# Local attention on one core: score tiles with 128 stationary columns in place of 82

## The chip, the cores and the metric

The kernel runs on one core of a Trainium2 chip. The metric is the device time of one execution in microseconds (us), as a median of repeated runs. A profiler's trace of one further execution shows what each engine did. The engines are TensorE (matmuls, PE in the profile, with its weight loads as PEld), VectorE (DVE), ScalarE (ACT), GpSimd (POOL) and SyncE (SP), which issues transfers.

A matmul on TensorE has two operands: the stationary one, which a weight load puts into the array of 128 rows by 128 columns, and the moving one, which is then streamed through column by column. In the profile a form such as `32*82 32x146` is a stationary operand of 32 rows and 82 columns and a moving one of 32 rows and 146 columns. Stationary columns become partitions of the result in PSUM. Where the operands have only 32 rows, a matmul uses one of four row strips of the array, and matmuls on different strips can run side by side.

## The reference

32 images and texts are embedded to 164 tokens each (36 of the image by a stem and a deformable convolution, 128 of the text by a quantized table), of width 192. Then comes one layer of local attention with 12 heads of 16, and a two-layer spline network. The attention is what the change touches:

```python
q = (x @ Wq + bq).reshape(B, N, H, d).transpose(0, 2, 1, 3)
k = (x @ Wk + bk).reshape(B, N, H, d).transpose(0, 2, 1, 3)
v = (x @ Wv + bv).reshape(B, N, H, d).transpose(0, 2, 1, 3)
scores = jnp.einsum('bhqd,bhkd->bhqk', q, k) * SCALE
allowed = jnp.abs(idx[:, None] - idx[None, :]) <= 64
scores = jnp.where(allowed[None, None], scores, -jnp.inf)
attn = jax.nn.softmax(scores, axis=-1)
out = jnp.einsum('bhqk,bhkd->bhqd', attn, v)
...
h = h + out @ Wo + bo
```

## The kernel before

The program has three stages that follow each other on the core: the tokens (stem, offsets, sampling, deformable convolution, text), the attention (`attend_phase`) and the spline network. The change is in the second, with some constants that the first loads and casts.

The attention works on pairs of sequences, 16 pairs, with a loop body for an even and an odd pair. A sequence's 164 tokens are split into two halves of 82 (`ROWS`). As a token sees at most 64 neighbours to each side, a half needs 82 + 64 = 146 (`SPAN`) columns on the other side of its scores. The 12 heads lie as 4 row strips of 32 partitions (j) times 3 groups (`HG`, g). Queries and keys are split into a high and a low part of type F32R (four bytes), so that scores need two passes: against `k1` and `k2`.

For each sequence TensorE computes the scores twice:

- by query (`queries_scores`), into the PSUM tile `scores_by_query` of two banks, in four blocks q = 0 to 3. A block covers one half of the tokens and two strips (strips 0 and 1 for even q, 2 and 3 for odd q): 12 matmuls that stream 146 columns (L1329), then 6 that add the mask (`add_mask`, L1352, which streams 96, 96 and 108 columns on each strip). VectorE then takes the maximum over the keys (L1021). There is one such tile: the next block waits until the maximum has read it.
- by key (`keys_scores`), into `scores_by_key` of four banks, in two blocks c = 0, 1. A block covers one half of the tokens and all four strips: 24 matmuls (L1364), 12 for the mask (L1352) and 12 that subtract the queries' maxima (L1374, with the stationary constant `pickr` and the moving transposed maxima `mT`). ScalarE then exponentiates (L1194).

The other matmuls of a round are the transposes of x and of the maxima (L1294, L1384), the projections to queries, keys and values (L1301 to L1305, L1313 to L1317), the weighted sums (`mix`, L1396) and the output projection (L1408). The order on TensorE is written out by hand in `pair`: while one sequence's scores by key are made, the next sequence's scores by query are made between them. In the first half of a pair's loop body (i = 0) the next pair's x is transposed and its queries and keys are projected; in the second half (i = 1) its values are. VectorE in the second half computes the layer statistics of the pair after the next (`norm_in`) ahead of the first maximum. `keep_going` issues matmuls whose result is not used, at the start and the end of the stage.

The stationary operands of the touched matmuls are 82 columns of `q1` (L1329), of `k1` and `k2` (L1364), of `piecer` (L1352) and all of `pickr` (L1374). Results lie on 82 partitions, and VectorE and ScalarE read these.

At the stage's start GpSimd fills buffers with constants (L978 to L983); each memset counts up `zeros_set`, and TensorE, VectorE, ScalarE and GpSimd wait for 6 of these. The constants `piece` and `pick` come by transfer in the first stage and are cast to F32R by VectorE (L470, L472).

Of the kernel before, what the change touches and what calls it, by code (L numbers as in the profile page):

```python
# [19 lines left out]
F32 = mybir.dt.float32  # L20
F32R = mybir.dt.float32r
# [4 lines left out]
P = 128  # L26
# [11 lines left out]
TOK = VIS + TXT  # L38
ROWS = TOK // 2
WINDOW = 64  # L40
SPAN = ROWS + WINDOW
# [3 lines left out]
PT = 2 * TOK  # L45
# [9 lines left out]
HEADS, DH = 12, 16  # L55
HG = HEADS // 4
# [56 lines left out]
class Constants:  # L113
# [4 lines left out]
    def __init__(self, nc, stack, a, front):  # L118
        sb, ps, sem = memories(nc, stack)
        self.pix_neg = sb("pixel_neg", [P, NPIXC + 1])  # L120
        self.ident = front.ident
        self.rows = sb("deform_rows", [P, 2, D])
        sizes = (("wq", HG * P), ("wk", HG * P), ("wv", D))
        self.high = [sb(f"attend_{k}_high", [P, 2, n], F32R) for k, n in sizes]
        self.low = [sb(f"attend_{k}_low", [P, 2, n], F32R) for k, n in sizes]
        self.piecer = sb("window_piece_r", [P, 2, SPAN], F32R)
        self.maskr = sb("window_mask_r", [P, 2, EDGE], F32R)
        self.pickr = sb("attend_pick_r", [P, HG, ROWS], F32R)
        self.minus_low = sb("attend_minus_low", [P, 2])
        self.xe = sb("attend_x_rest_ones", [P, PT], F32R)  # L130
        self.offset_in, self.pixel_in, self.attend_in = sem("offset_in"), sem("pixel_in"), sem("attend_const_in")
        self.dcn_in = sem("deform_in")

    def stage(self, nc, stack, a):

        sb = memories(nc, stack)[0]
        sizes = (("wq", HG * P), ("wk", HG * P), ("wv", D))
        self.off_w = sb("offset_weights", [P, TAPS, 2 * TAPS])
        self.off_bias = sb("offset_bias", [P, 1])
        self.off_grid = sb("offset_grid", [P, 8 * VIS])  # L140
        self.raw = [sb(f"attend_{k}", [P, 3, n]) for k, n in sizes]
        self.rest_low = sb("attend_rest_low", [P, 1])
        self.piece = sb("window_piece", [P, 2, SPAN])
        self.mask = sb("window_mask", [P, 2, EDGE])
        self.pick = sb("attend_pick", [P, HG, ROWS])
        self.ones_row = sb("attend_ones_row", [P, PT])
        self.loads = ((self.off_w[0:C1], a["off_w"], self.offset_in), (self.off_bias[:], a["off_bias"], self.offset_in),
                      (self.off_grid[:], a["off_grid"], self.offset_in), (self.ident[:], a["identity"], self.offset_in),
                      (self.pix_neg[0:PIXC], a["pix_neg"], self.pixel_in),
                      *((dst[:], a[k], self.attend_in) for dst, k in  # L150
                        ((self.raw[0], "wq"), (self.raw[1], "wk"), (self.raw[2], "wv"), (self.rest_low, "rest_low"), (self.mask, "mask"), (self.piece, "piece"), (self.pick, "pick"),
                         (self.minus_low, "minus_low"))))
        self.attend_count = 16 * (len(self.loads) - self.FIRST)
        self.loads += self.more
# [660 lines left out]
def attend_phase(nc, c, front, a, vis_scr, txt_scr, h_scr, w_raw, w1_in, total_scr, rec_scr):  # L815
# [14 lines left out]
    with ExitStack() as stack:  # L830
# [13 lines left out]
        q1, k1, k2 = ([sb(f"attend_{k}{u}", [P, HG, PT], F32R) for u in range(2)] for k in ("q1_", "k1_", "k2_"))  # L844
# [131 lines left out]
        def _(pool):  # L976
# [3 lines left out]
            pool.memset(prT[0:ROWS, 0, :, SPAN:TOK], 0.0).then_inc(zeros_set, 1)  # L980
            for u in range(2):
                pool.memset(va[u][:, :, :, 0:DH], 0.0).then_inc(zeros_set, 1)
                pool.memset(va[u][:, :, :, DH:32], 1.0).then_inc(zeros_set, 1)  # L983
            pool.wait_ge(half_set, 1)
            pool.wait_ge(zeros_set, 6)
# [14 lines left out]
        def _(dve):  # L1000
            dve.wait_ge(zeros_set, 6)
# [157 lines left out]
        def _(act):  # L1159
# [88 lines left out]
            act.wait_ge(zeros_set, 6)  # L1248
# [20 lines left out]
        def _(pe):  # L1269
# [49 lines left out]

            def queries_scores(a, u, i, q, first=False):  # L1320
# [4 lines left out]
                for g in range(HG):  # L1325
                    for k in (k1[u], k2[u]):
                        for j in range(2):
                            r = slice(64 * h + 32 * j, 64 * h + 32 * j + 32)
                            nc.tensor.matmul(sc[0:ROWS, j, g * SPAN:(g + 1) * SPAN],  # L1329
                                             q1[u][r, g, i * TOK + n * ROWS:i * TOK + (n + 1) * ROWS],  # L1330
# [4 lines left out]
            def add_mask(scores, n, tiles, stop):  # L1335

                for p in range(3):
                    for row, bank in tiles:
                        r = slice(32 * row, 32 * row + 32)
                        of = scores[0:ROWS, bank, 0:SW].rearrange("p (g n) -> p g n", n=SPAN)  # L1340
# [11 lines left out]
                        last = nc.tensor.matmul(to, piecer[r, n, at:at + ROWS], edge, start=False,  # L1352
# [3 lines left out]
            def keys_scores(a, u, i, c, most, first=False):  # L1356
# [3 lines left out]
                for g in range(HG):  # L1360
                    for k in (k1[u], k2[u]):
                        for j in range(4):
                            r = slice(32 * j, 32 * j + 32)
                            nc.tensor.matmul(tp[0:ROWS, j, g * SPAN:(g + 1) * SPAN],  # L1364
                                             k[r, g, i * TOK + c * ROWS:i * TOK + (c + 1) * ROWS],
                                             q1[u][r, g, i * TOK + FROM[c]:i * TOK + FROM[c] + SPAN],
                                             start=(g == 0 and k is k1[u]), stop=False)
# [3 lines left out]
                for g in range(HG):  # L1371
                    for j in range(4):
                        r = slice(32 * j, 32 * j + 32)
                        last = nc.tensor.matmul(tp[0:ROWS, j, g * SPAN:(g + 1) * SPAN], pickr[r, g, :],  # L1374
# [101 lines left out]
            pe.wait_ge(zeros_set, 6)  # L1476
# [505 lines left out]
def layouts(i):  # L1982
# [55 lines left out]
    for j, (conv, bn) in enumerate((("stem", "bn1"), ("dcn", "bn2"))):  # L2038
# [11 lines left out]
        "pick": np.tile(-(row % DH == group).astype(f32)[..., None], (1, 1, ROWS)),  # L2050
# [4 lines left out]
        "piece": np.tile(np.stack([piece, piece[:, ::-1]], 1).astype(f32), (4, 1, 1)),  # L2055
# [25 lines left out]
```

## Time and profile before

| what | value |
|---|---|
| median of 3 runs | 2442.05 us (2440.94 to 2452.29) |
| the profiled execution | 2410.74 us, its span 2409.0 us |
| mean granted TensorE clock | 0.974 |
| TensorE matmuls busy | 2301.1 us (96%), 19971 instructions |
| weight loads busy | 2153.2 us (89%) |
| VectorE busy | 1878.0 us (78%) |
| ScalarE busy | 1397.2 us (58%) |
| GpSimd busy | 229.8 us (10%) |

The span runs from the first to the last instruction of the program, and the profiled execution's own time is 1.7 us longer. Busy times are unions of the instructions' intervals; since matmuls are pipelined and overlap, a busy TensorE is not one at its peak, and the pace is read from the starts of instructions that follow each other. The granted clock is the share of TensorE's full clock that its throttle let through. A wait is written behind the instruction that it held up, with what ended it.

### The profile page before, as it was taken

To read this page: it belongs to the slowest core of one execution; us is meant where nothing else is said; L and a number is where in the kernel's file an instruction comes from. 1 tells how busy PE (TensorE), PEld (TensorE's weight loads), DVE (VectorE), ACT (ScalarE), POOL (GpSimd) and SP (SyncE) were. 2 spreads that over 40 slices of the span, in tenths; PEclk is the share of its full clock that TensorE was granted. 3 is DMA by queue.
4 is the path that set the end of the run, shared out by engine and by line. 5 is a ranking of instruction groups with operands and counts; after the bars stand their busy time and mean duration, and the time that the engine had idled before them with its cause. 6 is when DMAs were issued, how large, how long until landed. Compare 5 with 4: busy or idle time off the path is not lost.

```text
span 2409.0 us, 48738 instructions
## 1 busy us (share of the span) xinstructions
PE 2301.1 (96%) x19971; PEld 2153.2 (89%) x19971; DVE 1878.0 (78%) x2364; ACT 1397.2 (58%) x1391; POOL 229.8 (10%) x133
## 2 busy tenths in 40 slices
PE   7699989999999889999999999989999999999999
PEld 6466877777777789999999999989999999999999
DVE  8799755666666487766766767689999999999995
ACT  5689113444444554435435344588888888888881
POOL 5522000000000021211211111000000000000000
PEclk9899997999999899999999999999999999999999
DMA  7655131111111100000000000210000000000000
GB/s 238 178 149 152 47 142 34 45 47 44 47 47 44 37 22 27 20 15 26 20 24 19 19 26 24 90 59 23 24 22 23 23 23 23 23 23 23 23 19 10
DMA packets 99326, 115.82 MB, mean 48 GB/s; under 512 B 15271, under 2 KB 90551, under 8 KB 98487
## 3 DMA queue, kind: packets, MB, share of 16 engines
q1 hardware_dynamic: 79087, 89.38, 12.3%
q10 hardware_dynamic: 16520, 14.34, 2.0%
q0 software_dynamic: 3616, 10.54, 1.7%
q8 instruction: 87, 1.43, 0.2%
q14 instruction: 16, 0.13, 0.0%
HBM read 83.36 MB, written 30.86 MB: 47 GB/s over the span
## 4 chain that ended last, share of the span: by engine, by line
PE 64%; issue 0%; DVE 0%
PE spline_acc L1915 27%; PE spline_acc L1888 10%; PE spline_acc L1887 10%; PE spline_acc L1889 10%; PE spline_acc L1909 5%; PE spline_acc L1911 2%; PE spline_xT L764 0%; DVE spline_f L1664 0%; DVE spline_weights_low L1647 0%; DVE spline_x L1734 0%; DVE spline_x L1737 0%
## 5 line engine op out<-in xcount | busy, mean ns | idle before, releaser
L1915 PE MATMUL spline_acc<-spline_weights,spline_f 128*128 128x192 f32 x3936 | 672.2, 328 | 0.0
L1915 PEld LDWEIGHTS spline_acc<-spline_weights,spline_f 128*128 128x128 f32 x3936 | 637.4, 190 | 0.0
L1887 PE MATMUL spline_acc<-spline_f,spline_weights_high 128*128 128x328 f32 x1536 | 480.5, 313 | 2.5 <-DVE spline_weights_low L1647 2.5
L1888 PE MATMUL spline_acc<-spline_f,spline_weights_high 128*128 128x328 f32 x1536 | 481.2, 313 | 0.0
L1889 PE MATMUL spline_acc<-spline_f,spline_weights_low 128*128 128x328 f32 x1536 | 477.7, 311 | 0.0
L1887 PEld LDWEIGHTS spline_acc<-spline_f,spline_weights_high 128*128 128x128 f32 x1536 | 289.1, 188 | 2.8 <-DVE spline_weights_low L1647 2.8
L1889 PEld LDWEIGHTS spline_acc<-spline_f,spline_weights_low 128*128 128x128 f32 x1536 | 289.3, 188 | 0.0
L1888 PEld LDWEIGHTS spline_acc<-spline_f,spline_weights_high 128*128 128x128 f32 x1536 | 289.3, 188 | 0.0
L1909 PE MATMUL spline_acc<-spline_weights_split,spline_f_high 128*128 128x384 f32 x656 | 218.2, 389 | 8.2 <-issue 8.2
L1664 DVE SCALAR_TENSOR_TENSOR spline_f<-spline_front 128x984 fp32r<-128x984 f32 x128 | 145.6, 1178 | 100.2 <-PE spline_acc L1889 94.9
L1021 DVE TENSOR_REDUCE attend_max<-scores_by_query 82x6 f32<-82x876 f32 x128 | 136.3, 1065 | 57.5 <-PE scores_by_query L1352 56.8
L1817 ACT ACTIVATE spline_hid<-spline_acc 128x328 f32<-128x328 f32 x64 | 28.2, 445 | 243.6 <-PE spline_acc L1889 243.6
L1911 PE MATMUL spline_acc<-spline_weights_split,spline_f_low 128*128 128x192 f32 x656 | 164.6, 251 | 0.0
L1194 ACT ACTIVATE attend_probs<-scores_by_key 82x1752 f32<-82x1752 f32 x64 | 104.3, 1630 | 93.2 <-PE scores_by_key L1374 93.2
L1664 DVE SCALAR_TENSOR_TENSOR spline_f<-spline_n,spline_a 128x984 fp32r<-128x984 f32 x64 | 75.6, 1181 | 99.7 <-PE spline_acc L1889 98.9
L1675 DVE SCALAR_TENSOR_TENSOR spline_f<-spline_front 128x1536 f32<-128x1536 f32 x84 | 147.0, 1750 | 0.0
L1675 DVE SCALAR_TENSOR_TENSOR spline_f<-spline_n,spline_b 128x1536 f32<-128x1536 f32 x80 | 140.0, 1750 | 0.0
L1909 PEld LDWEIGHTS spline_acc<-spline_weights_split,spline_f_high 128*128 128x128 f32 x656 | 124.0, 189 | 8.5 <-issue 8.5
L1911 PEld LDWEIGHTS spline_acc<-spline_weights_split,spline_f_low 128*128 128x128 f32 x656 | 125.7, 192 | 0.0
L574 ACT ACTIVATE spline_front<-spline_front,pixel_neg 120x576 f32<-120x576 f32 x160 | 109.7, 763 | 12.4 <-DMA spline_front<-pos_scr 11.1
L1782 ACT ACTIVATE spline_s<-spline_xn,spline_offset 128x512 f32<-128x512 f32 x160 | 101.9, 708 | 7.9 <-DMA spline_xn<-hid_scr 6.4
L1329 PEld LDWEIGHTS scores_by_query<-attend_k,attend_q 32*82 32x82 f32 x1536 | 69.6, 154 | 41.0 <-DVE attend_max L1021 25.2
(229 smaller groups left out, 4266.6 us busy)
## 6 DMA issues: line engine op xcount, KB each, us to landing
spline_front<-pos_scr SPq DMA_DIRECT2D x32, 540.0 KB, 4.4
hid_scr<-spline_hid SPq DMA_DIRECT2D x64, 164.0 KB, 1.8
spline_xn<-hid_scr SPq DMA_DIRECT2D x41, 256.0 KB, 3.1
attend_spread<-rec_scr SPq DMA_DIRECT2D x128, 61.5 KB, 2.1
pix_scr<-spline_front SPq DMA_DIRECT2D x32, 225.0 KB, 3.8
spline_weights_raw<-w SPq DMA_DIRECT2D x1, 6144.0 KB, 21.4
spline_weights<-w SPq DMA_DIRECT2D x4, 1536.0 KB, 6.2
spline_x<-h_scr SPq DMA_DIRECT2D x41, 96.0 KB, 1.9
```

The source lines that it names most:

```text
L574: nc.scalar.activation(dy[u][0:PIXC, part, :].rearrange("p (k n) -> p k n", k=TAPS), p[:, 0], ACT.Abs, bias=neg[0:PIXC, part:part + 1])
L1021: nc.vector.tensor_reduce(mx[0:ROWS, n, 2 * h:2 * h + 2, 0:HG], sc[0:ROWS, :, 0:SW].rearrange("p j (g n) -> p j g n", n=SPAN), AX_X, ALU.m ...
L1194: nc.scalar.activation(prT[0:ROWS, c, :, FROM[c]:FROM[c] + SPAN].rearrange("p (j g) n -> p j g n", j=4), tp[0:ROWS, :, 0:SW].rearrange("p ...
L1664: nc.vector.scalar_tensor_tensor(f[j % RING][:, part * HC:(part + 1) * HC], n_[u][:, cols], MAGIC + i, v[:, cols], ALU.is_equal, ALU.mult) ...
L1675: nc.vector.scalar_tensor_tensor(dst[:], n, MAGIC + i, v, ALU.is_equal, ALU.mult).then_inc(f_ready, 1)
L1782: nc.scalar.activation(dst[:, r * HID:(r + 1) * HID].rearrange("p (c n) -> p c n", c=CH), x2[u], ACT.Identity, bias=bias2[:, r:r + 1], sca ...
L1887: nc.tensor.matmul(z, high, x_high, start=start, stop=False)
L1888: nc.tensor.matmul(z, high, x_low, start=False, stop=False)
L1889: last = nc.tensor.matmul(z, low, x_high, start=False, stop=stop)
L1909: nc.tensor.matmul(acc2[:, u, 0:2 * D], f_high[i][:, cols], w2_split[:, i, r].rearrange("p s o -> p (s o)"), start=start, stop=False)
L1911: last = nc.tensor.matmul(z, f_low[i][:, cols], w2_split[:, i, r, 0, :], start=False, stop=False)
L1915: last = nc.tensor.matmul(z, f_rest[i][:, cols], w2[:, i, r, :], start=False, stop=stop)
```

## The change

The stationary operands of all score, mask and maximum matmuls grow from 82 to 128 columns. What is streamed stays. The results have 46 more partitions, which nobody reads. As the 128 columns from the last position of a buffer would reach past its end, `q1`, `k1` and `k2` (two buffers each) get 46 further columns behind their three groups; elsewhere the further columns are those of the neighbouring tokens or of the next group. The tails are filled with zeros by six more memsets on GpSimd, and the waits on `zeros_set` go from 6 to 12. `piecer` grows from 146 to 192 columns a half, padded with zeros, and `pickr` from 82 to 128 a group.

```diff
-        self.piecer = sb("window_piece_r", [P, 2, SPAN], F32R)
+        self.piecer = sb("window_piece_r", [P, 2, WINDOW + P], F32R)
-        self.pickr = sb("attend_pick_r", [P, HG, ROWS], F32R)
+        self.pickr = sb("attend_pick_r", [P, HG, P], F32R)
...
-        q1, k1, k2 = ([sb(f"attend_{k}{u}", [P, HG, PT], F32R) for u in range(2)] for k in ("q1_", "k1_", "k2_"))
+        wide = {k: [sb(f"attend_{k}{u}", [P, HG * PT + P - ROWS], F32R) for u in range(2)] for k in ("q1_", "k1_", "k2_")}
+        q1, k1, k2 = ([y[:, 0:HG * PT].rearrange("p (g n) -> p g n", g=HG) for y in wide[k]] for k in ("q1_", "k1_", "k2_"))
...
+            for y in wide["q1_"] + wide["k1_"] + wide["k2_"]:
+                pool.memset(y[:, HG * PT:].bitcast(F32), 0.0).then_inc(zeros_set, 1)
...
-            pool.wait_ge(zeros_set, 6)
+            pool.wait_ge(zeros_set, 12)
...
+            def columns(k, u, r, g, at):
+
+                at += g * PT
+                return wide[k][u][r, at:at + P]
+
...
-                            nc.tensor.matmul(sc[0:ROWS, j, g * SPAN:(g + 1) * SPAN],
-                                             q1[u][r, g, i * TOK + n * ROWS:i * TOK + (n + 1) * ROWS],
+                            nc.tensor.matmul(sc[:, j, g * SPAN:(g + 1) * SPAN],
+                                             columns("q1_", u, r, g, i * TOK + n * ROWS),
...
-                        last = nc.tensor.matmul(to, piecer[r, n, at:at + ROWS], edge, start=False,
+                        last = nc.tensor.matmul(to, piecer[r, n, at:at + P], edge, start=False,
...
-                            nc.tensor.matmul(tp[0:ROWS, j, g * SPAN:(g + 1) * SPAN],
-                                             k[r, g, i * TOK + c * ROWS:i * TOK + (c + 1) * ROWS],
+                            nc.tensor.matmul(tp[:, j, g * SPAN:(g + 1) * SPAN],
+                                             columns(k, u, r, g, i * TOK + c * ROWS),
...
-                        last = nc.tensor.matmul(tp[0:ROWS, j, g * SPAN:(g + 1) * SPAN], pickr[r, g, :],
+                        last = nc.tensor.matmul(tp[:, j, g * SPAN:(g + 1) * SPAN], pickr[r, g, :],
```

## Rows read from the trace of the kernel before

**Rows 1.** Busy time by window: the attention stage; columns: us, busy (x instructions), granted clock, DMA.

```profile
337.00:838.00 501.00, 461.61 (x8261) 392.35 (x8257) 307.98 (x674) 208.34 (x302) 17.03 (x17) 0.93 0.15 42
```

**Rows 2.** The same view: one round at full clock, one with a half-clock stretch.

```profile
591.40:620.60 29.20, 27.11 (x519) 23.16 (x518) 19.65 (x44) 12.93 (x19) 1.00 (x1) 1.00 0.17 47
558.10:591.40 33.30, 31.42 (x520) 26.48 (x519) 19.68 (x45) 12.92 (x19) 1.00 (x1) 0.85 0.16 41
```

**Rows 3.** Groups of weight loads by shape: count | busy us, mean ns | idle before.

```profile
L1329 PEld LDWEIGHTS scores_by_query<-attend_k,attend_q 32*82 32x82 f32 x1536 | 69.6, 154 | 41.0 <-DVE attend_max L1021 25.2 <-issue 15.7
...
L1352 PEld LDWEIGHTS scores_by_query<-window_mask_r,window_piece_r 32*82 32x82 f32 x768 | 40.4, 154 | 0.0
L1364 PEld LDWEIGHTS scores_by_key<-attend_q,attend_k 32*82 32x82 f32 x1536 | 39.4, 157 | 8.8 <-issue 3.9 <-ACT attend_probs L1194 1.9
...
L1352 PEld LDWEIGHTS scores_by_key<-window_mask_r,window_piece_r 32*82 32x82 f32 x768 | 24.7, 160 | 0.0
L1374 PEld LDWEIGHTS scores_by_key<-attend_max_split,attend_pick_r 32*82 32x82 f32 x768 | 24.5, 159 | 4.8 <-DVE attend_max_split L1035 4.6
```

**Rows 4.** Timeline of weight loads, a key and a query block: start, us.

```profile
646.17 0.52 PEld L1364 LDWEIGHTS scores_by_key<-attend_q,attend_k 32*82 32x82 f32 x24 [0.20 <-issue]
646.60 0.30 PEld L1352 LDWEIGHTS scores_by_key<-window_mask_r,window_piece_r 32*82 32x82 f32 x12
...
647.32 0.54 PEld L1329 LDWEIGHTS scores_by_query<-attend_k,attend_q 32*82 32x82 f32 x12 [0.19 <-issue]
647.75 0.33 PEld L1352 LDWEIGHTS scores_by_query<-window_mask_r,window_piece_r 32*82 32x82 f32 x6
```

**Rows 5.** The same timeline: loads of 128 and of 82 columns following each other.

```profile
643.13 0.19 PEld L1301 LDWEIGHTS attend_spare<-attend_x_high,attend_wk_high 128*128 128x128 f32 x1 [0.65 <-ACT attend_mixed L1187]
643.24 0.19 PEld L1302 LDWEIGHTS attend_spare<-attend_x_low,attend_wk_high 128*128 128x128 f32 x1
...
653.76 0.15 PEld L1313 LDWEIGHTS attend_spare<-attend_wv_high,attend_x_high 128*82 128x82 f32 x1
653.83 0.15 PEld L1314 LDWEIGHTS attend_spare<-attend_wv_low,attend_x_high 128*82 128x82 f32 x1
653.92 0.15 PEld L1315 LDWEIGHTS attend_spare<-attend_wv_high,attend_x_low 128*82 128x82 f32 x1
...
671.80 0.20 PEld L1384 LDWEIGHTS attend_spare<-identity_all,attend_max 82*128 82x128 f32 x2 [0.23 <-issue]
```

**Rows 6.** Timeline of weight loads at half clock.

```profile
566.44 0.54 PEld L1352 LDWEIGHTS scores_by_query<-window_mask_r,window_piece_r 32*82 32x82 f32 x6
```

**Rows 7.** Timeline of TensorE's matmuls: the waits of one round.

```profile
650.94 0.66 PE L1329 MATMUL scores_by_query<-attend_k,attend_q 32*82 32x146 f32 x12 [0.61 <-DVE attend_max L1021]
...
652.97 0.66 PE L1329 MATMUL scores_by_query<-attend_k,attend_q 32*82 32x146 f32 x12 [0.27 <-DVE attend_max L1021]
...
659.79 0.45 PE L1374 MATMUL scores_by_key<-attend_max_split,attend_pick_r 32*82 32x146 f32 x12 [0.25 <-DVE attend_max_split L1035]
...
666.66 0.39 PE L1301 MATMUL attend_spare<-attend_x_high,attend_wq_high 128*128 128x328 f32 x1 [0.49 <-DVE attend_x_rest L1044]
```

**Rows 8.** Timeline of VectorE in the same round.

```profile
649.82 1.07 DVE L1021 TENSOR_REDUCE attend_max<-scores_by_query 82x6 f32<-82x876 f32 x1
```

**Rows 9.** Busy time by window: before and in a half-clock stretch.

```profile
558.00:562.00 4.00, 3.08 (x88) 2.56 (x86) 2.69 (x4) 0.99 (x1) 1.00 (x1) 1.00 0.25 68
562.00:572.00 10.00, 10.00 (x128) 8.06 (x124) 4.76 (x13) 2.39 (x5) 0.00 (x0) 0.50 0.14 44
```

**Rows 10.** Timeline of all engines at the stage's start.

```profile
314.92 0.74 POOL L983 MEMSET attend_v<- 128x768 f32 x1
...
319.62 1.14 DVE L668 BATCH_NORM_STATS2 attend_stats<-attend_x 82x6 f32<-82x192 f32 x4 [9.47 <-DMA attend_x<-txt_scr]
```

**Rows 11.** Timeline of VectorE where the constants are cast.

```profile
64.49 0.31 DVE L470 CAST window_piece_r<-window_piece 128x292 fp32r<-128x292 f32 x1 [3.55 <-DMA attend_minus_low<-minus_low]
...
69.86 0.52 DVE L480 SCALAR_TENSOR_TENSOR spline_front<-offset_acc,offset_bias,offset_grid 128x288 f32<-128x288 f32 x1 [1.20 <-PE offset_acc L447]
```

More of the change, by code:

```diff
@@ L142, in stage @@
         self.rest_low = sb("attend_rest_low", [P, 1])
-        self.piece = sb("window_piece", [P, 2, SPAN])
+        self.piece = sb("window_piece", [P, 2, WINDOW + P])
         self.mask = sb("window_mask", [P, 2, EDGE])
-        self.pick = sb("attend_pick", [P, HG, ROWS])
+        self.pick = sb("attend_pick", [P, HG, P])
         self.ones_row = sb("attend_ones_row", [P, PT])
@@ L1000, in _ @@
         def _(dve):
-            dve.wait_ge(zeros_set, 6)
+            dve.wait_ge(zeros_set, 12)
             def norm_in(tt, u):
@@ L1247, in _ @@
                 high(k1[0][:, g, :], start(START["K"][g]))
-            act.wait_ge(zeros_set, 6)
+            act.wait_ge(zeros_set, 12)
             for i in range(2):
@@ L1339, in add_mask @@
                         r = slice(32 * row, 32 * row + 32)
-                        of = scores[0:ROWS, bank, 0:SW].rearrange("p (g n) -> p g n", n=SPAN)
+                        of = scores[:, bank, 0:SW].rearrange("p (g n) -> p g n", n=SPAN)
                         if p < 2:
@@ L1360, in keys_scores @@
                 for g in range(HG):
-                    for k in (k1[u], k2[u]):
+                    for k in ("k1_", "k2_"):
                         for j in range(4):
                             r = slice(32 * j, 32 * j + 32)
-                            nc.tensor.matmul(tp[0:ROWS, j, g * SPAN:(g + 1) * SPAN],
-                                             k[r, g, i * TOK + c * ROWS:i * TOK + (c + 1) * ROWS],
+                            nc.tensor.matmul(tp[:, j, g * SPAN:(g + 1) * SPAN],
+                                             columns(k, u, r, g, i * TOK + c * ROWS),
                                              q1[u][r, g, i * TOK + FROM[c]:i * TOK + FROM[c] + SPAN],
-                                             start=(g == 0 and k is k1[u]), stop=False)
+                                             start=(g == 0 and k == "k1_"), stop=False)
                 add_mask(tp, c, [(j, j) for j in range(4)], False)
@@ L1475, in _ @@
             keep_going(48, tp[:, 0, 0:HG * P])
-            pe.wait_ge(zeros_set, 6)
+            pe.wait_ge(zeros_set, 12)
             for j in range(2):
@@ L2049, in layouts @@
         "wo": wo.reshape(P, HG, D),
-        "pick": np.tile(-(row % DH == group).astype(f32)[..., None], (1, 1, ROWS)),
+        "pick": np.tile(-(row % DH == group).astype(f32)[..., None], (1, 1, P)),
         "minus_low": -np.concatenate([row % 32 >= DH, row % 32 >= DH], 1).astype(f32),
@@ L2054, in layouts @@
         "mask": np.tile(np.where(np.stack([mask, mirror], 1), NEG, 0.0).astype(f32), (4, 1, 1)),
-        "piece": np.tile(np.stack([piece, piece[:, ::-1]], 1).astype(f32), (4, 1, 1)),
+        "piece": np.tile(np.pad(np.stack([piece, piece[:, ::-1]], 1), ((0, 0), (0, 0), (0, P - ROWS))).astype(f32), (4, 1, 1)),
         "patches": x.reshape(B, 3, HS, K, HS, K).transpose(1, 3, 5, 0, 2, 4).reshape(PATCH, B, PIX),
```

## The prediction, made before the result was known

> **What bounds the kernel now.** The page of the profile comes first: TensorE is busy for 96% of the span, and the chain that ended last runs almost wholly through its matmuls. The change touches one stage alone, so I cut the span into stages and look at the windows: from 337 to 838 us the attention runs, 501 us long, with TensorE busy for 462 of them, VectorE for 308 and ScalarE for 208 [rows 1]. The other two stages keep their instructions, apart from the preparations costed below.
>
> Next, one steady round of the stage's loop, a pair of sequences of 164 tokens: 29.20 us at the full clock, 33.30 us where a stretch at half clock fell into it [rows 2]. The reader is to see that the same 519 or 520 instructions take 4.1 us more there.
>
> Then the weight loads of the touched lines by shape [rows 3]. The five groups hold 1536 + 768 + 1536 + 768 + 768 loads, all of 32 rows by 82 columns. Queries' scores use two row strips of the array at once, keys' scores four. I call one load on each strip in use a step: 1536/2 + 768/2 + 1536/4 + 768/4 + 768/4 = 1920 steps, 60 for each of 32 sequences: four query blocks of 9 steps and two key blocks of 12.
>
> How long is a step? In the load timeline, L1364's 24 loads (6 steps) begin at 646.17 and L1352's at 646.60: 72 ns a step. L1329's 12 loads (6 steps) begin at 647.32, L1352's at 647.75: 72 ns again, with half as many strips [rows 4]. The mask steps, whose matmuls stream 96 or 108 columns and not 146, are no shorter: six loads take 0.33 us from the first's start to the last's end, one takes 0.15, and the 0.18 between are two steps and the offset of the second strip [rows 4, 5]. At half clock the same 6 mask loads take 0.54 [rows 6]. So a step does not follow what is streamed; it follows something that halves with the clock and is the same for 96 and 146 columns. The load itself is the candidate.
>
> **What a load of 128 columns costs.** Where nothing streams yet and two loads follow each other, the second begins as soon as the first lets it. With 82 columns that is 0.07 us (653.76 to 653.83); with 128 columns, of the same four-byte type as the changed tiles, 0.11 us (643.13 to 643.24) [rows 5]. These are loads on all 128 rows, the nearest rows there are; the trace has no load of 32 rows by 128 columns. The 0.07 agrees with the 72 ns of a strip's step, so I take the same difference for the strips: +0.04 us a step. Scaling 72 ns by 128/82 gives 112, the same 0.04. At half clock it is 0.08. The other bound is zero or a gain: two loads of 128 columns for a transpose (L1384) fit into 0.20 us, where the pair at 643.13 needs 0.11 + 0.19 = 0.30 [rows 5]. That is a transposing matmul on plain F32; the changed ones are ordinary matmuls on F32R, as the pair at 643.13, so I go with the latter.
>
> The Trainium skill speaks against this: its page "TensorE: Matmul & The Clock Gate", section on weight-path perf modes, says that fast weight load comes on when there are exactly 128 weights and the type is not FP32. The same section grants no win to 32-bit weights. The F32R loads at 643.13, 0.11 us apart, do not show it at work; no run here shows it on strips of 32 rows. By that rule the sum would be that of the first rival below, and not the one that follows.
>
> **The sum.** All 1920 steps at +0.04 are 77 us. What of it is on the path is read from one round, engine by engine.
>
> *Second sequence's half, from 646.17.* The first key block (12 steps, +0.48) and first query block (9, +0.36) end before the next query block, which starts at 650.94 after 0.61 us idle, released by VectorE's maximum [rows 7]. That maximum began only at 649.82, 1.7 us after the scores it reads were streamed at about 648.1; VectorE had the next pair's layer statistics to do first [rows 4, 8]. In between stands the output projection, which ends 0.61 us before 650.94. The scores can come 0.84 later. The projection slips by 0.84 less the 0.19 that the loads at 647.32 stood idle [rows 4]: 0.65 against 0.61, so nothing worth counting is late. If that cover were gone, 0.65 us a round. The later three query blocks are in line with everything: 3 x 0.36. The second key block runs while VectorE takes the maximum of block two; TensorE waits 0.27 us for that anyway, at 652.97, and part of the block runs on strips the queries do not use [rows 7]. Its release is already late by the 0.36 counted, so of 0.48 I count nothing. Sum 1.08.
>
> *First sequence's half.* The key block waits 0.25 us (TensorE) for the split maxima at 659.79 [rows 7]; its nine steps before that (+0.36) overrun the wait by 0.11 at most, which I leave to the range. Its three steps after it: 0.12. Four query blocks 4 x 0.36 = 1.44, second key block 0.48. Against it the wait of 0.49 for VectorE's low part of x at 666.66 goes [rows 7]: VectorE's chain to it moves by 0.36 (through one maximum), TensorE by 0.84. Sum 0.12 + 1.44 + 0.48 - 0.49 = 1.55.
>
> Together 2.63 of 4.80 us a round, 55%; 16 rounds make 42 us. The four query blocks ahead of the first round (+1.4) and the three that the last one lacks (-1.1) cancel.
>
> *The clock.* The stage's mean granted clock is 0.93 [rows 1]; with the two levels 1.0 and 0.5 that is 14% of 501 us, 70 us, at half clock. A stretch of 10 us there holds 128 matmuls [rows 9], against 519 in 29.20 [rows 2]: 0.72 of the pace, so 10% of the steps, 192. There TensorE is busy for 10.00 of 10, and each step costs 0.08, uncovered: 15 us. The other nine tenths: 0.9 x 42 = 38. Sum 53 if the falls stay as they are. The two in steady rounds begin at about 562 and 743; the first follows a stretch in which TensorE was busy for only 3.08 of 4 us [rows 9], the second looks alike; most of the missing time is the wait for the maximum, which the change fills. I take it that these two go: 2 x 4.1 back, and their 20 of the 70 us cost 4 less. **53 - 8 - 4 = +41 us.**
>
> *The rest.* Six more memsets of 46 columns on GpSimd stand ahead of the release of all engines (12 counts in place of 6). The last of today's begins at 314.92 and takes 0.74; VectorE waits until 319.62 for x by DMA [rows 10], 4 us of cover for what a memset of 768 columns sets at 0.74 each, six of 46 at well under 1 us in all. Two constants grow, 292 to 384 and 246 to 384 columns (118 KB more by DMA), and their casts (0.31 for 292 columns) by some 0.2; VectorE idles 1.20 us for TensorE soon after [rows 11]. Both cost nothing; uncovered, about 1 us each. Matmul counts, streamed columns, semaphores and what the other engines read stay.
>
> **The rivals.** *A fast load.* If strips load 128 columns in under 0.07, streaming sets the step. Matmuls of 192 columns follow at 0.09 (653.83 to 653.92) [rows 5], 0.47 ns a column: 68 ns for 146, 45 for 96, 51 for 108. A query block then takes 549 in place of 657 ns, a key block 753 in place of 876: 1.36 a round, 12 us at the 55% above, 22 at all of it, and up to 8 more from the falls. Middle -20: 2422 us. For it speaks L1384, against it L1301. It decides from the point where the load is shorter than today's 72 ns.
>
> *The clock stays full all through.* 70 us at half clock cost 0.41 of their length by [rows 2] (4.1 of 10), 29 us; 42 - 29 = +13: 2455. For it: the waits get filled. Against: some stretches fall outside steady rounds.
>
> *Nothing hides.* Maximum and projection chains slip with TensorE, or falls come oftener (4.1 each): 0.9 x 77 + 15 = +84: 2526.
>
> *The step is not the load's* but a fixed cost of a strip: 0, 2442. Against it stands that 0.07 and 0.11 differ at all.
>
> **How the numbers follow.** The profiled execution took 2410.74 us, 31.3 less than the median 2442.05; I carry the difference of +41 over: 2483. Chances: load-bound and half hidden (+20 to +65) 0.63; nothing hides 0.11; clock stays full 0.10; fast load 0.10; no change 0.06. Half a per cent, 12 us, is about what a measurement of this kernel can tell from none. Slower: the first two and a little of the third, 0.76; same: no change and half of the clock's, 0.12; faster: 0.12. The range leaves out the fast load, the case of no change and the top of "nothing hides": 2447 to 2520.
>
> **What the profile would show.** Right: touched loads 0.11 apart, key steps at 646 to 647 stretched by half; rounds of 31.8 us in place of 29.2; waits before L1329 and L1301 shorter; the stage near 540 us, the others as before. Wrong: steps still 72 ns or less, rounds shorter than 29.2, or the stage's mean clock at 1.0.

## The result, and the profile after

| | before | after |
|---|---|---|
| median of 6 runs | 2439.78 us (2412.88 to 2452.29) | 2516.70 us (2507.41 to 2532.74) |
| the profiled execution, its span | 2410.74, 2409.0 us | 2532.74, 2531.1 us |
| its mean granted clock | 0.974 | 0.943 |

The ratio is 1.0354 (95% interval 1.0308 to 1.0399): slower, as forecast, and inside the range; but the medians moved by 77 us where 41 were forecast. The ratio compares the fast runs of the two kernels alone and is not the quotient of the two medians (1.0315).

First the step. In the timeline of the weight loads of the kernel after (start, us, engine, line, then the tiles), the 24 loads of the keys' scores (now L1372) begin at 533.01 and the mask's at 533.68: 0.67 us for 6 steps, 0.11 a step where [rows 4] have 0.07.

```profile
524.25 0.74 PEld L1337 LDWEIGHTS scores_by_query<-attend_k,attend_q 32*128 32x128 f32 x12 [0.44 <-DVE attend_max L1024]
...
526.62 0.74 PEld L1337 LDWEIGHTS scores_by_query<-attend_k,attend_q 32*128 32x128 f32 x12
527.28 0.41 PEld L1360 LDWEIGHTS scores_by_query<-window_mask_r,window_piece_r 32*128 32x128 f32 x6
...
533.01 0.75 PEld L1372 LDWEIGHTS scores_by_key<-attend_q,attend_k 32*128 32x128 f32 x24
533.68 0.42 PEld L1360 LDWEIGHTS scores_by_key<-window_mask_r,window_piece_r 32*128 32x128 f32 x12
...
571.87 1.40 PEld L1337 LDWEIGHTS scores_by_query<-attend_k,attend_q 32*128 32x128 f32 x12
573.15 0.76 PEld L1360 LDWEIGHTS scores_by_query<-window_mask_r,window_piece_r 32*128 32x128 f32 x6
```

Two strips at 526.62 (queries, now L1337) give 0.66 for 6 steps, the same 0.11. At half clock, from 571.87, they take 1.28: 0.21 a step. The same block at half clock in the kernel before takes 0.84, 0.14 a step, so there the change costs 0.07 a step:

```profile
383.91 0.96 PEld L1329 LDWEIGHTS scores_by_query<-attend_k,attend_q 32*82 32x82 f32 x12
384.75 0.54 PEld L1352 LDWEIGHTS scores_by_query<-window_mask_r,window_piece_r 32*82 32x82 f32 x6
```

Now the rounds, in the view of busy time by window (us, then PE, PEld, DVE, ACT and POOL busy with their instructions, granted clock, DMA): ten steady rounds; one at full clock; the next; and in that one the stretch before its fall of the clock, and the fall. Last, all that lies ahead of the attention.

```profile
523.13:881.43 358.30, 350.04 (x5182) 306.82 (x5181) 198.70 (x431) 129.11 (x190) 10.02 (x10) 0.88 0.14 38
523.13:555.17 32.04, 31.21 (x521) 27.65 (x520) 19.95 (x45) 12.92 (x19) 1.00 (x1) 1.00 0.15 43
555.17:594.83 39.66, 38.79 (x519) 33.69 (x518) 19.79 (x45) 12.91 (x19) 1.00 (x1) 0.78 0.13 35
555.20:559.60 4.40, 4.25 (x90) 3.88 (x88) 2.60 (x4) 0.70 (x1) 1.00 (x1) 1.00 0.36 90
559.60:576.70 17.10, 17.10 (x169) 14.50 (x168) 6.13 (x14) 4.30 (x6) 0.00 (x0) 0.50 0.10 29
0.00:355.00 355.00, 295.27 (x1635) 212.61 (x1637) 277.27 (x359) 192.19 (x306) 120.95 (x92) 0.92 0.53 152
```

The same ten rounds and the same first 355 us of the kernel before:

```profile
470.33:771.99 301.66, 279.92 (x5182) 238.37 (x5181) 196.79 (x432) 129.26 (x190) 10.04 (x10) 0.97 0.17 46
...
0.00:355.00 355.00, 306.20 (x1845) 227.69 (x1846) 287.04 (x384) 194.28 (x308) 101.49 (x87) 0.95 0.54 154
```

A full-clock round takes 32.04 us, 2.84 more than the 29.20 of [rows 2]. But every other round takes 39.66, since the clock falls to half for 17.1 us in it. The falls of the ten rounds begin at 559.6, 631.3, 703.0, 774.7 and 846.3: 71.7 apart, which is one round of each kind. Before, two stretches of 10 us fell into ten rounds, at 4.1 each. So of the 56.6 us that ten rounds gained (358.30 less 301.66), 28.4 are ten full-clock rounds' 2.84, and the clock's share is 5 x 7.62 less 2 x 4.1, 30; the two make 58. The whole stage, from the first query scores to the last weighted sums, went from 493.1 us (336.5 to 829.6) to 598.8 (354.6 to 953.3), where the prediction's sum gave some 40 more.

What stands ahead of a fall is new too. In [rows 9] TensorE was busy for 3.08 of the 4 us before it; here for 4.25 of 4.40. Its timeline shows, behind the output projection that ends at 556.1, query block, key block and query block with no gap but 0.15:

```profile
556.29 0.89 PE L1337 MATMUL scores_by_query<-attend_k,attend_q 32*128 32x146 f32 x12 [0.15 <-DVE attend_max L1024]
...
558.66 0.89 PE L1337 MATMUL scores_by_query<-attend_k,attend_q 32*128 32x146 f32 x12
559.40 0.60 PE L1360 MATMUL scores_by_query<-window_mask_r,window_piece_r 32*128 32x96 f32 x6
559.93 0.45 PE L1316 MATMUL attend_spare<-attend_wv_high,attend_x_high 128*82 128x192 f32 x1
```

The Trainium skill, page "TensorE: Matmul & The Clock Gate", section "HAM oscillation — how this bites in real kernels", describes a kernel whose clock falls in TensorE's waits for transfers between bursts of matmuls. No such wait stands ahead of this fall: the wait of 0.61 is down to 0.15, and the fall comes all the same.

**How much of the 77 is the clock.** Executions of one kernel differ mainly in it. The 47 runs of the kernel before that stand beside this study's runs reach from clock 0.960 to 0.975; with an execution's half-clock time taken as 2 x (1 - clock) x span, a straight line through them costs 0.41 us per us of it (the clock is given to 0.001, which is 5 us). Their median, 0.967, is 160 us at half clock; the six runs of after have 0.9495, 254 us. So 94 x 0.41 = 38 us of the 77 are clock, and 39 are left for the loads. This is an estimate: the line is carried on from at most some 195 us at half clock to 254, though the six runs of after, taken alone, give 0.415 too. Against the 47 runs' own median time, 2435.5 us, the difference is 81, and 43 are left; 16 rounds of 2.84 are 45.

The profiled executions differ by 122 us, and 18 of these lie ahead of the attention (336.5 against 354.6 us up to the first L1329 or L1337). That is not the change: with the 82 columns of before, the profiled execution of e7 below has the same 0.92 there and 355.5 us.

```profile
0.00:355.00 355.00, 294.78 (x1623) 211.68 (x1624) 277.18 (x359) 191.61 (x305) 121.52 (x86) 0.92 0.53 152
```

### The profile page after: what moved, and what is told of

The parts are those of the page before. It is cut to its first block, busy times and chain, and to the rows that moved or that the text cites. A ratio compares the mean times of both kernels' runs of the same rounds, so it can differ in the third digit from the quotient of the medians.

```text
span 2531.1 us, 48744 instructions
## 1 busy us (share of the span) xinstructions
PE 2433.3 (96%) x19971; PEld 2275.7 (90%) x19971; DVE 1880.5 (74%) x2364; ACT 1397.0 (55%) x1391; POOL 249.7 (10%) x139
## 4 chain that ended last, share of the span: by engine, by line
PE 60%; issue 0%; DVE 0%
PE spline_acc L1923 25%; PE spline_acc L1896 9%; PE spline_acc L1895 9%; PE spline_acc L1897 9%; PE spline_acc L1917 5%; PE spline_acc L1919 2%; PE spline_xT L764 0%; DVE spline_f L1672 0%; DVE spline_weights_low L1655 0%; DVE spline_x L1742 0%; DVE spline_x L1745 0%
## 5 line engine op out<-in xcount | busy, mean ns | idle before, releaser
L1024 DVE TENSOR_REDUCE attend_max<-scores_by_query 82x6 f32<-82x876 f32 x128 | 136.6, 1067 | 134.9 <-PE scores_by_query L1360 133.4
L1337 PEld LDWEIGHTS scores_by_query<-attend_k,attend_q 32*128 32x128 f32 x1536 | 110.5, 212 | 24.7 <-issue 14.1
L1337 PE MATMUL scores_by_query<-attend_k,attend_q 32*128 32x146 f32 x1536 | 127.2, 303 | 5.2 <-DVE attend_max L1024 3.8
```

The source lines that it names most:

```text
L1024: nc.vector.tensor_reduce(mx[0:ROWS, n, 2 * h:2 * h + 2, 0:HG], sc[0:ROWS, :, 0:SW].rearrange("p j (g n) -> p j g n", n=SPAN), AX_X, ALU.m ...
L1337: nc.tensor.matmul(sc[:, j, g * SPAN:(g + 1) * SPAN], columns("q1_", u, r, g, i * TOK + n * ROWS), k[r, g, i * TOK + FROM[n]:i * TOK + FRO ...
```

## The experiments

The theory after the result: the load's step costs 2.84 us a round, whatever the clock does; the other half is the clock, which falls more often and longer because of what the slower loads make of a sequence in the second half in which nothing but strip matmuls runs: second query block, second key block, third query block. It is called the strip run below. The rival: the whole time comes from the loads, half clock being only where they are dearer. In the table, "ten rounds" are ten steady rounds with their mean clock and their time at half clock, "round" one at full clock, both from the one execution of each kernel that was traced. Each ratio is to runs of before made beside that kernel's own, whose median is not always the 2439.78 of the first row.

| kernel | median us | ratio to before (95%) | ten rounds, clock, at half | round |
|---|---|---|---|---|
| before | 2439.78 | | 301.66, 0.97, 20.5 | 29.20 |
| after | 2516.70 | 1.0354 (1.0308 to 1.0399) | 358.30, 0.88, 85 | 32.04 |
| e1 96 columns | 2476.92 | 1.0184 (1.0122 to 1.0247) | 314.04, 0.95, 34 | 29.96 |
| e2 queries alone | 2479.77 | 1.0200 (1.0137 to 1.0263) | 336.29, 0.92, 51 | 31.47 |
| e3 keys alone | 2481.73 | 1.0182 (1.0114 to 1.025) | 336.05, 0.88, 79 | 29.59 |
| e4 after, values early | 2559.37 | none | 376.66, 0.84, 120 | |
| e5 after, fill in the strip run | 2486.18 | 1.0212 (1.0155 to 1.0269) | 329.85, 0.99, 3.4 | 32.89 |
| e6 after, fill elsewhere | 2484.06 | 1.0232 (1.0168 to 1.0296) | 332.91, 0.97, 17 | 32.56 |
| e7 before, fill in the wait | 2425.62 | 0.9964 (0.9929 to 0.9998) | 300.54, 0.98, 14 | 29.22 |
| e8 before, values early | 2445.74 | 1.0052 (1.0012 to 1.0092) | 331.41, 0.86, 96 | |
| e9 after, 1 elsewhere | 2546.94 | 1.0463 (1.0393 to 1.0534) | 369.31, 0.85, 109 | 32.21 |
| e10 after, 6 elsewhere | 2517.66 | 1.0333 (1.0256 to 1.0409) | 353.74, 0.93, 51 | 33.10 |
| e11 after, e5 and 3 elsewhere | 2484.61 | 1.0223 (1.0153 to 1.0293) | 333.49, 1.00, 0 | 33.36 |
| e12 before, two fills | 2417.10 | 0.9936 (0.9902 to 0.9971) | 297.14, 1.00, 0 | 29.42 |

**e1: 96 columns in all touched matmuls.**

```diff
-                return wide[k][u][r, at:at + P]
+                return wide[k][u][r, at:at + 96]
...
-                        last = nc.tensor.matmul(to, piecer[r, n, at:at + P], edge, start=False,
+                        last = nc.tensor.matmul(to, piecer[r, n, at:at + 96], edge, start=False,
```

The results' partitions and `pickr` are cut to 96 likewise.

> All touched matmuls have 96 stationary columns in place of 128; the 14 more than 82 are not read. Theory (the step is the load, about 0.85 ns a column; and a long starved stretch on the strips lets the clock fall): a step takes 0.083 to 0.085 us, between 0.073 at 82 and 0.111 at 128; a round at full clock about 30.0 us, 0.8 more than before; 13 us over the kernel before, and at most a few stretches of half clock more. Rival one (the fourth quadrant of result partitions costs, 82 and 96 both fill three): a step as before, 0.073, and the time within 0.5% of before. Rival two (the falls are a matter of the round's length against the chip's own rhythm): step as the theory, but falls as often as with 128 columns or not at all, whatever the load.

The load timeline of e1:

```profile
577.66 0.59 PEld L1372 LDWEIGHTS scores_by_key<-attend_q,attend_k 32*96 32x96 f32 x24
578.16 0.34 PEld L1360 LDWEIGHTS scores_by_key<-window_mask_r,window_piece_r 32*96 32x96 f32 x12
```

0.50 for 6 steps, 0.083: between 0.072 (82) and 0.111 (128), about 0.86 ns a column, so the step follows the columns loaded. The round, 29.96, is 0.76 longer than before; 14 of 46 columns of 2.84 are 0.86. The time was missed: 41 us over the before beside it (2476.92 against 2435.90) where 13 were expected. 16 rounds of 0.76 are 12 of them, and with a median clock of 0.9525 its runs had some 75 us more at half clock than before's, which by 0.41 are 31.

**e2 and e3: 128 columns for the queries' scores and their masks alone, or for the keys' alone.** The helper `columns` and `add_mask` take the width; here e2.

```diff
-                                             columns(k, u, r, g, i * TOK + c * ROWS),
+                                             columns(k, u, r, g, i * TOK + c * ROWS, ROWS),
...
-                add_mask(tp, c, [(j, j) for j in range(4)], False)
+                add_mask(tp, c, [(j, j) for j in range(4)], False, ROWS)
```

> Only the scores by query and their masks have 128 stationary columns; scores by key, their masks and the maxima have 82. Theory: query steps 0.111, key steps 0.073; a round at full clock about +2.1 us over 29.2 (seven blocks of nine steps count, less the wait for x that goes); the half-clock stretch after the second key block comes less often than with all 128. Rival two: as many falls as with all 128. Time 30 to 60 us over before.

> Only the scores by key, their masks and the subtracted maxima have 128 stationary columns; scores by query have 82. Theory: key steps 0.111, query steps 0.073; the first key block of each half hides behind VectorE, so a round at full clock is only 0.5 to 0.9 us over 29.2; 10 to 20 us over before without more falls. If nothing hid it would be 4 x 0.46 = 1.8 a round.

At full clock the queries cost 31.47 - 29.20 = 2.27 a round and the keys 0.39; together 2.66 of the 2.84. My sum of the seven query blocks, 7 x 0.36, was 2.52; the keys' 0.12 + 0.48, less the wait of 0.49 that goes, 0.11. So the hiding was read about rightly. But the ten rounds of e2 and e3 are equally long, since e3 has 79 us at half clock and e2 51; e3 is 46 us over the before beside it, where 10 to 20 were expected.

The falls of the two differ in place. The three of e2 begin at the end of the strip run, as those of after do. Of e3's five, one does (583.4); the other four (532.2, 634.6, 737.0, 805.2) begin at a second place, in the first half, behind its second key block and third query block, where TensorE waits for the low part of x. That wait is 0.49 in [rows 7]; here it is 1.4 to 2.2 us:

```profile
531.89 0.39 PE L1304 MATMUL attend_spare<-attend_x_high,attend_wq_high 128*128 128x328 f32 x1 [2.23 <-DVE attend_x_rest L1047]
```

So most of e3's half-clock time stands behind a wait, and is not shown to be the keys' loads in the strip run.

**e4: after, with the next values' projection moved into the strip run, between query block 2 and the key block of the second half.**

```diff
+                        if q == 1 and i == 1 and more:
+                            values(0, use(t, V[0]))
...
-                                if more:
-                                    values(0, use(t, V[0]))
```

> The changed kernel (128 columns everywhere) with one move: in the second half of a round the first ten value projections, full-array matmuls, are issued between the second query block and the second key block and no longer behind the third query block. Theory: steps stay 0.111 and a full-clock round near 32, but the stretch of strips that precedes each fall is broken up, and the half-clock stretches of the steady rounds (one every second round, 7.6 us each) go: about 50 us less than the changed kernel, near 2465. Rival two: the falls stay as often, somewhere else in the round; time within 10 us of the changed kernel.

The falls went on: 120 us of ten rounds at half clock, where they were expected to go. Its runs lie too far apart (2523 to 2586 us) for a ratio; none is faster than after's fastest. The falls come later in the round, behind a new run that the move made; one begins at 564.3, within the mask's matmuls of L1360:

```profile
561.11 0.83 PE L1337 MATMUL scores_by_query<-attend_k,attend_q 32*128 32x146 f32 x12
...
562.19 1.04 PE L1404 MATMUL attend_spare<-attend_probs,attend_v 82*32 82x164 f32 x24
563.42 0.89 PE L1337 MATMUL scores_by_query<-attend_k,attend_q 32*128 32x146 f32 x12 [0.19 <-DVE attend_max L1024]
564.16 0.63 PE L1360 MATMUL scores_by_query<-window_mask_r,window_piece_r 32*128 32x96 f32 x6
564.72 0.72 PE L1404 MATMUL attend_spare<-attend_probs,attend_v 82*32 82x146 f32 x8
```

Between 561 and 564 stand scores, then `mix` on 82 rows and 32 columns, then scores: with the projection gone from its old place, nothing there uses all 128 rows of the array.

**e5 and e6: after, with three matmuls of `keep_going` (128 rows, 128 columns, 384 streamed, result unused) in the strip run, and, as a control, the same three elsewhere, ahead of the keys' projections.**

```diff
+                        if q == 1 and i == 1 and more:
+                            keep_going(3, xb[:, claim(use(t, V[0])), 0:HG * P])
```
```diff
+                        keep_going(3, xb[:, claim(use(t, K_[0])), 0:HG * P])
                         for g in range(HG):
```

> The changed kernel with three more full-array matmuls of 384 columns (0.52 us, result not used) between the second query block and the second key block of a round's second half; nothing is moved. Theory (the clock falls after the run of strip work there: query block, key block, query block, whose matmuls stream for less of the time since each waits for a longer load): the half-clock stretches of the steady rounds go, a full-clock round is 32.0 to 32.5, every round is one, and the time is about 45 us under the changed kernel, near 2470. Rival two (only the round's length against the chip's rhythm): falls as often or changed without regard to the place, time within 15 us of the changed kernel.

> The changed kernel with the same three matmuls, but ahead of the three key projections in the first half of a round, among other full-array work. It is the control of the run before: the round grows by the same 0.52 us. Theory: the falls stay where they were, after the strip work, about every second round; time 0 to 20 us over the changed kernel. Rival two: the same effect as of the run before, whichever way that went.

The ten rounds of e5, then of e6:

```profile
511.33:841.18 329.85, 321.58 (x5212) 282.85 (x5211) 198.74 (x431) 129.13 (x190) 10.03 (x10) 0.99 0.15 42
```

```profile
496.35:829.26 332.91, 323.86 (x5212) 287.66 (x5211) 198.79 (x432) 129.24 (x190) 10.05 (x10) 0.97 0.16 41
```

With 30 matmuls more, ten rounds of e5 are 28 us shorter than after's; one fall of 3.4 us is left, at the second place (695.5) with no wait ahead of it. Its median is 30 us below after's although each round is 0.85 longer: that half of the loss was the clock, not the loads. But the control does nearly the same, against what was expected of it, and by the clocks of all their runs (medians 0.970 and 0.968) the two cannot be told apart. In e6 the fall that remains begins at the old place (566.4), so the place is still open to falls; they come less often. Either the dense work helps wherever it stands, or a round's length (32.56 against 32.04) decides which rounds fall. e9 to e11 ask that.

**e9 and e10: the control with 1 and with 6 matmuls. e11: e5's three and e6's three together.**

```diff
+                        keep_going(1, xb[:, claim(use(t, K_[0])), 0:HG * P])
```

> The changed kernel with one full-array matmul of 384 columns (0.17 us) ahead of the key projections, away from the strip work. The theory is now in two parts: the run of strip work in the second half makes a fall possible, and how the round's length stands to the chip's own rhythm decides how often one happens; in the changed kernel two rounds and one fall of 17 us come out so that the next fall meets the same place. Then 0.17 us a round is enough to change the count: full-clock rounds near 32.2, falls in steady rounds still only behind that strip work, but not one in every second round; 10 to 70 us at half clock in ten steady rounds. If the place alone decides, they stay at about 85.

> The same with six such matmuls (1.04 us). Theory: full-clock rounds near 33.0, the length of the round of run 5, but with the strip work unbroken: some falls, behind the third query block of the second half; 15 to 85 us at half clock in ten steady rounds. If the length alone made run 5 free of falls, this one is free of them too.

> The changed kernel with three matmuls in the strip work (as run 5) and three more ahead of the key projections (as run 6). Theory: full-clock rounds near 33.4, and as in run 5 no fall behind the strip work whatever the length; under 10 us at half clock in ten steady rounds. If run 5 was free of falls by its length alone, falls come back, 20 us or more.

The ten rounds of e9, e10 and e11:

```profile
504.61:873.92 369.31, 361.37 (x5192) 318.33 (x5191) 198.78 (x432) 129.45 (x190) 10.05 (x10) 0.85 0.14 37
```

```profile
517.20:870.94 353.74, 344.71 (x5242) 305.28 (x5241) 198.70 (x431) 129.22 (x190) 10.05 (x10) 0.93 0.14 39
```

```profile
499.42:832.91 333.49, 324.45 (x5242) 286.72 (x5241) 198.73 (x431) 129.25 (x190) 10.04 (x10) 1.00 0.15 41
```

With 0, 1, 3 and 6 matmuls elsewhere, ten rounds have 85, 109, 17 and 51 us at half clock, and the median clocks of all their runs (0.9495, 0.9405, 0.968, 0.959) rank them alike. For e9, 10 to 70 us had been expected. More dense work outside the strip run is not steadily better, so it is not that work as such. Inside the strip run, three matmuls leave 3.4 us (e5), and 0 with a round 0.47 longer (e11). That the place of the fill counts beside the length rests mainly on e10 and e11, whose rounds are near in length (33.10 and 33.36) and whose median clocks are 0.959 and 0.973. The falls of e10 come every fourth round at one place (522.1, 662.1, 802.0), as those of e2 do (527.3, 660.4, 793.5); e1's every fifth (505.6, 662.6, 819.6).

**e7 and e8: before, with three such matmuls in the wait of 0.61 us ahead of query block 2 [rows 7], or with the values' projection moved there.**

```diff
+                        if q == 0 and i == 1 and more:
+                            keep_going(3, xb[:, claim(use(t, V[0])), 0:HG * P])
```

> The kernel before (82 columns) with three such matmuls in the 0.6 us that TensorE waits for the maximum ahead of the second query block. Theory: a round at full clock stays 29.2 to 29.3, as the wait covers them; the half-clock stretches that follow this place in the kernel before (two in steady rounds of the profiled execution, more in slower executions) go; 8 to 20 us faster than before. If the wait has no part in the falls: no difference.

> The kernel before (82 columns) with the first ten value projections issued in that same wait, ahead of the second query block, and no longer behind the third query block. A round at full clock gets some 0.5 us shorter (0.9 us of work into 0.6 of waiting). If only loads of 128 columns let the clock fall, 8 us or more faster than before. If any long run of strip work does, as the run with the same move in the changed kernel (4) suggests, more half-clock stretches than before, now after the third query block, and a time 0 to 30 us over before.

e7's fill lies in a wait and costs nothing (29.22); it is 0.4% faster, hardly to be told from no change. In its ten rounds no fall begins at the old place; the one there is (676.2) begins at the second, behind a wait of 1.47 us. e8 is the surprise: the work that filled the wait made the falls more, not fewer, with 82 columns and no change to any load: 96 us at half clock in ten rounds.

```profile
480.87:812.28 331.41, 311.59 (x5182) 265.98 (x5181) 197.05 (x432) 128.56 (x190) 10.03 (x10) 0.86 0.15 41
```

This execution was one of the slower of its kernel, as that of before was one of the faster: the median clocks are 0.960 and 0.967, some 35 us at half clock apart. Of the nine falls five begin where the values stood. That, as in e4, matmuls on part of the rows are left alone there may be why; no run tests it by itself. The other four begin at the second place, behind waits of 1.1 to 1.6 us:

```profile
531.40 0.39 PE L1301 MATMUL attend_spare<-attend_x_high,attend_wq_high 128*128 128x328 f32 x1 [1.46 <-DVE attend_x_rest L1044]
```

So filling the wait of 0.61 does not by itself hold the clock, loads of 128 columns are not needed for falls, and at the second place falls do stand behind waits.

**e12: before, with e7's fill and two matmuls ahead of the first half's second key block, which leads to the second place.** The wait on `exped` is that of the key block itself, taken earlier.

```diff
+                            if q == 2 and i == 0 and more and not first:
+                                pe.wait_ge(exped, 2 * a + 1)
+                                keep_going(2, tp[:, 0, 0:HG * P])
                             keys_scores(a, u, i, q // 2, most, first and i == 0)
...
+                        if q == 0 and i == 1 and more:
+                            keep_going(3, xb[:, claim(use(t, V[0])), 0:HG * P])
```

> The kernel before (82 columns) with the fill of run 7 and two more such matmuls ahead of the second key block of the first half, where TensorE later waits 0.49 us for x. A round at full clock 29.2 to 29.4; falls in steady rounds fewer than in run 7, under 10 us in ten rounds; 10 to 20 us faster than before if the falls behind the second place count, else as run 7, 0.4% faster.

```profile
483.83:780.97 297.14, 280.12 (x5232) 239.50 (x5231) 196.71 (x431) 128.93 (x190) 10.04 (x10) 1.00 0.17 46
```

No fall in ten rounds, though waits for x of up to 1.08 us remain, and with 2417.1 us over 12 runs (ratio 0.9936, 0.9902 to 0.9971) it beats both kernels, by 0.6% over the one before. Beside e11, also without a fall, it gives the loads' price with the clock left out: ten rounds differ by 36.4 us, of which the fills make 10 x (1.32 - 0.22), and 25 are left, 2.5 a round.

## Why the prediction was half right

- **The step**: right. +0.04 us at full clock (0.072 to 0.111), and the 0.08 for half clock was 0.07 (0.14 to 0.21). The load binds, and it follows the columns (e1). The rivals of a fast load and of a step that is not the load's fall. By the Trainium skill, page "TensorE: Matmul & The Clock Gate", section "Weight-path perf modes — Fast Weight Load (FWL) and DoubleRow", 128 weights that are not FP32 load fast; the trace does not agree for F32R on strips of 32 rows, with 0.111 a step at 128 columns against 0.083 at 96. The same section grants 32-bit weights no win, and with that the trace agrees.
- **What hides it**: right, 2.84 us a round against 2.63, and by the estimate above 39 to 43 us over the program against the 42 of the sum. The waits of 0.27, 0.25 and 0.49 of [rows 7] are gone after, as counted; that of 0.61 is 0.15 at 556.29 (PE) and 0.44 at 524.25 (PEld). The cover went over to VectorE: L1024 now waits 134.9 us in all, 133.4 of them for the scores' masks; in the kernel before (L1021) it waited 57.5.

```profile
L1021 DVE TENSOR_REDUCE attend_max<-scores_by_query 82x6 f32<-82x876 f32 x128 | 136.3, 1065 | 57.5 <-PE scores_by_query L1352 56.8
L1024 DVE TENSOR_REDUCE attend_max<-scores_by_query 82x6 f32<-82x876 f32 x128 | 136.6, 1067 | 134.9 <-PE scores_by_query L1360 133.4
```

- **The clock**: this is the step that failed. "I take it that these two go", the falls of steady rounds, rested on one row, the wait that stood ahead of them; as the change would fill it, I gave 12 us back. The clock's terms (0.9 of 42, +15, -8, -4) summed to -1. Measured they are +38: the falls come in every other round and last 17.1 us, not 10.2. That the wait's filling with strip matmuls does not stop them is shown by after itself (PE busy 4.25 of 4.40). With full-array matmuls in that wait (e7, e12) no fall begins there in ten rounds, but before had only two to lose. That the falls, and not the loads, are that half of the loss is shown by e5, e6 and e11, which keep the loads and lose all falls of ten rounds or all but one. The rival "Nothing hides" had as its second half that falls come oftener; that came, and its first half did not.
- **The profiled execution**: its 31.3 us below the median were carried over as a constant. Some 14 of them are half-clock time (0.974 against a median of 0.967 is 34 us at half clock, by 0.41), so they were no constant: the profiled execution of after is the slowest of its six.
- **The rest**: the first stage's memsets, constants and casts show nothing that can be told from its clock; behind the attention the span keeps its 1578 us (1579.4 before, 1577.7 after).

**What stays open.** In the ten rounds of every kernel here the falls begin in or shortly behind matmuls that use part of the array's rows: in the strip run, behind the weighted sums (e4, e8) or at the second place, and breaking the strip run with three full-array matmuls leaves 3.4 of 85 us. But which rounds fall hangs on something else as well, most likely their length (e6, e9, e10), and two kernels that only moved work on 128 rows (e4, e8) made new places for falls. At the second place a wait may be the reason, but waits of up to 1.26 us there were also passed without a fall (e3, e7, e12), and e5's fall had none. How much of the extra half-clock time comes from the longer loads in the strip run and how much from the new length of the round is not separated: no run has the longer loads at a round of 29.20.

## What to carry to other kernels

Stationary columns beyond those needed are not free where the load sets the pace: price them by the step between loads, and read which waits cover it, engine by engine. Treat the clock as a term with its own unknown sign: a wait that stood ahead of one fall is no proof that filling it stops the fall. Where a stage has a long run on strips, try a few full-array matmuls in it or in a wait beside it, and compare executions at their granted clock before a difference is put down to anything else.

## What the runs showed of the hardware

- The clock fell to half with TensorE busy for 4.25 of the 4.40 us before, the last 3.3 of them with matmuls on 32-row strips, and in these traces the falls kept step with the loop: every 71.7 us in after, one round of 32.04 and one of 39.66; every fourth or fifth round in e1, e2 and e10.
- Three matmuls of 128 rows by 128 columns, 0.5 to 0.9 us a round, put into the strip run took away 82 of 85 us at half clock in ten rounds (e5); elsewhere they took away 68 (e6).
- Loads of 32 rows take 0.072, 0.083 and 0.111 us a step for 82, 96 and 128 columns, the same on two strips as on four: four strips load side by side. At half clock a step takes 0.13 to 0.14 at 82 columns and 0.21 at 128.
- Nine falls of e3, e7 and e8 began in or up to 1.2 us behind a wait of TensorE of 1.1 to 2.2 us.
- Between runs of one kernel the clock moved from 0.960 to 0.975, which by 0.41 is some 30 us of 2440.
